# Layers two and three of a Fourier tower: where a pair's forward column transform stands among its products

## The reference, cut to what matters

```python
for i in range(nl):                                   # nl = 4
    h_ft = jnp.fft.rfft2(h)
    w_c = spec_wr[i] + 1j * spec_wi[i]
    out_modes = jnp.einsum('bixy,ioxy->boxy', h_ft[:, :, :mx, :my], w_c)   # 16 x 16 modes
    spec = jnp.fft.irfft2(out_modes, s=(H, W))
    conv = lax.conv_general_dilated(h, conv_w[i], (1, 1), 'SAME', dimension_numbers=dn)
    conv = conv + conv_b[i][None, :, None, None]
    h = leaky(spec + conv)
```

## Time and profile before

| | |
|---|---|
| median of 3 runs | 1116.0 us (1110.08, 1116.0, 1121.34) |
| the profiled execution's own time | 1121.72 us |
| span in its profile, first to last instruction | 1119.6 us |
| TensorE busy (matmul) | 1052.7 us, 94% |
| VectorE, ScalarE, GpSimd busy | 603.7, 466.2, 152.8 us |
| mean granted TensorE clock | 0.99 |

### The profile page before, as it was taken

The page is one execution under the profiler, slowest core; times in us unless marked ns, Lnnn a source line. Parts: engine busy times, 40 slices in busy tenths (PEclk is TensorE's granted clock), DMA queues, the critical chain, the costliest instruction groups (busy, mean ns, idle before and its releaser), DMA issues.

```text
span 1119.6 us, 48730 instructions
## 1 busy us (share of the span) xinstructions
PE 1052.7 (94%) x22512; PEld 553.4 (49%) x22512; DVE 603.7 (54%) x560; ACT 466.2 (42%) x895; POOL 152.8 (14%) x299
## 2 busy tenths in 40 slices
PE   5899999899999999899999998999999999899985
PEld 2555554555555554545544555434434344466743
DVE  5677788655556666555555665301233213387844
ACT  3355665223333333133333342223453534666524
POOL 2012221011111111011111110112102121200000
PEclk9999999999999999999999999999999999999998
DMA  9298889379888988588989887578757463000001
GB/s 321 62 206 209 211 189 256 106 213 272 252 254 257 267 212 241 150 243 222 269 251 261 241 236 191 135 171 193 179 143 167 102 142 83 7 4 1 1 1 19
DMA packets 66714, 194.27 MB, mean 174 GB/s; under 512 B 22256, under 2 KB 24816, under 8 KB 59248
## 3 DMA queue, kind: packets, MB, share of 16 engines
q1 hardware_dynamic: 54224, 138.19, 46.4%
q0 software_dynamic: 12288, 52.97, 17.3%
HBM read 138.13 MB, written 52.95 MB: 171 GB/s over the span
## 4 chain that ended last, share of the span: by engine, by line
PE 86%; DVE 6%; issue 4%; ACT 3%; DMA 0%; DVEq 0%; ACTq 0%
PE psum L662 16%; PE psum L648 15%; PE psum L694 12%; PE psum L676 7%; PE psum L633 5%; PE psum L620 5%; PE psum L566 4%; PE psum L553 4%; PE psum L712 3%; PE psum L605 2%; PE psum L908 2%; PE psum L720 1%; PE psum L760 1%; DVE xt L1288 1%; PE psum L926 1%
## 5 line engine op out<-in xcount | busy, mean ns | idle before, releaser
L1097 ACT ACTIVATE x_now<-psum,conv_bias 128x512 f32<-128x512 f32 x256 | 157.0, 691 | 340.3 <-PE psum L676 252.8
L1317 DVE STREAM_TRANSPOSE vt<-psum 128x1024 f32<-128x1024 f32 x64 | 126.2, 1972 | 195.1 <-PE psum L620 195.1
L1288 DVE STREAM_TRANSPOSE xt<-x_now 128x1024 f32<-128x1024 f32 x100 | 199.3, 2031 | 15.4 <-ACT x_now L1097 8.9
L1294 DVE STREAM_TRANSPOSE ft<-psum 128x1024 f32<-128x1024 f32 x50 | 100.8, 2016 | 194.0 <-PE psum L553 194.0
L662 PE MATMUL psum<-halo,conv 64*32 64x512 f32 x3072 | 188.3, 593 | 4.2 <-issue 4.2
L648 PE MATMUL psum<-halo,conv 128*128 128x512 f32 x384 | 179.7, 609 | 0.8 <-ACT x_now L1097 0.7
L497 POOL DMA_DIRECT2D activations<-x_now x192 | 94.3, 492 | 601.2 <-PE psum L662 411.6
L346 ACT ACTIVATE spec<-psum 32x128 f32<-32x128 f32 x372 | 143.7, 386 | 72.5 <-PE psum L566 68.7
L694 PEld LDWEIGHTS psum<-dft,vt 64*64 64x64 f32 x8192 | 130.3, 135 | 78.4 <-issue 77.1
L694 PE MATMUL psum<-dft,vt 64*64 64x64 f32 x8192 | 146.0, 221 | 4.4 <-issue 4.4
L648 PEld LDWEIGHTS psum<-halo,conv 128*128 128x128 f32 x384 | 69.0, 190 | 86.5 <-issue 78.1
(11 more groups left out here) (158 smaller groups left out, 793.7 us busy)
## 6 DMA issues: line engine op xcount, KB each, us to landing
halo<-activations SPq DMA_DIRECT2D x768, 132.0 KB, 3.5
activations<-x_now POOLq DMA_DIRECT2D x192, 264.0 KB, 4.1
wspec<-in_spec SPq DMA_DIRECT2D x64, 256.0 KB, 5.5
xcol<-in_xcol SPq DMA_DIRECT2D x16, 384.0 KB, 5.3
x_now<-in_ser SPq DMA_DIRECT2D x2, 1024.0 KB, 6.9
spec<-in_onehot SPq DMA_DIRECT2D x8, 256.0 KB, 5.7
wspec<-in_causal SPq DMA_DIRECT2D x8, 256.0 KB, 6.4
consts<-in_tail SPq DMA_DIRECT2D x6, 185.0 KB, 5.6
```

What stands on the lines that cost most here:

```text
L1097: copy(x_now[:, k, 16 * u:16 * u + 16, 0:G], acc[u].rearrange("p (i j) -> p i j", j=G), ACT.Prelu, bias=conv_bias[:, l:l + 1], alpha=SLOPE ...
L1288: vec.transpose(xt[:, 32 * m:32 * m + 32, :], src).then_inc(s_xt, 1)
L1317: vec.transpose(vt[:, k].rearrange("p h r o -> p (h r) o").rearrange("p y o -> p o y"), backed.rearrange("p a b -> p (a b)").rearrange("p ...
```

## The change

In `pair`, `columns_forward(T)` is issued after the second of the four centre products of pair `T` itself, from pair 2 on; the call at the end of the preceding pair is gone. At the boundaries into layers 2 and 3 it stands after the second centre product too, as it did at the boundary into layer 1. On ScalarE `spectrum` of a pair now stands ahead of the evictions of the pair in which its columns are computed, and no longer behind the evictions of the pair before; only the layer's last one keeps its old place. The number of instructions on each engine is unchanged, and no DMA, SyncE or GpSimd instruction is edited.

```diff
@@ -813,8 +813,10 @@
                     for part in range(4):
                         spectral(T, part)
                     return
-                for u in units(T):
+                for i, u in enumerate(units(T)):
                     convolve_centre(T, u)
+                    if p > 1 and i == 1:
+                        columns_forward(T)
                 for part in range(4):
                     spectral(T, part)
                 convolve_rows(T, 0)
@@ -824,7 +826,6 @@
                 convolve_columns(T, 1)
                 if p < LAST:
                     columns_back(T + 1)
-                columns_forward(T + 1)
 
             def last_pair(p):
 
@@ -858,7 +859,7 @@
                 T = l * PAIRS
                 for i, u in enumerate(units(T - 1)):
                     convolve_centre(T, u)
-                    if l == 1 and i == 1:
+                    if i == 1:
                         columns_forward(T)
                 rows_forward(T + 1)
                 convolve_rows(T, 0)
@@ -1176,7 +1177,7 @@
                         if u == 2:
                             fronts(p, 1)
                         head_activate(p - 1, u)
-                if l == 0 and p > 1:
+                if not last and p > 1:
                     spectrum(T - 2)
                 for u in units(T):
                     evict(T, u)
@@ -1187,7 +1188,7 @@
                     head_activate(p, 1)
                 if last:
                     fronts(p, 2)
-                if not last and (p > 0 if l > 0 else p == LAST):
+                if not last and p == LAST:
                     spectrum(T - 1)
                 if p == LAST and not last:
                     last_spectrum(T)
```

## The result

Over 20 runs of each kernel the changed one has a median of 1121.21 us (1117.76 to 1127.87) against 1116.99 us (1109.27 to 1123.04). The ratio is 1.0042 with a 95% interval of 1.0026 to 1.0058: 4.7 us more, between 2.9 and 6.5. The forecast was 6.5 us more, and 1122.5 us. The profiled execution took 1121.34 us, with a span of 1119.2.

The account below looks back on a forecast made before the run. TensorE, busy 94% and never waiting inside pairs, was taken as the bound. Splits (5.6 us) plus boundary waits (0.9) made +6.5 us on a median of 1116.0, so 1122.5 us, range 1115 to 1130.

Parts of the forecast that it names:

- TensorE waits for nothing in a pair, so there is no wait to win.: Pair ends of layers 1 and 2: ft is ready 0.34 us early, so 28 pair ends have no wait to remove.
- One more split costs 0.20 us.: Pairs 2 to 15 of two layers: a second run of whole-array products adds 0.20 us a pair, 5.6 us in all.
- The term L620 to L648: In a pair, columns_back before the first centre product: no change from 1.01 us, judged by L620 to L633 at 1.02.
- the second rival: Entering whole-array products from L620 costs another 0.20 us a pair: 12.1 us more, 1128 us, over 1% slower; chance 0.14.
- Evictions, `vt`, copies and `rows_forward` have time in hand in the pairs.: Inside pairs: no new waits, with at least 0.9 us in hand for evictions and 4 us for rows_forward.
- The boundaries make a wait of 0.44 us each.: Boundaries into layers 2 and 3: rows_forward waits for spec and starts 0.44 us later, 0.9 us for both.
- `convolve_columns` to the first centre product: Boundary into layer 2: 1.71 us plus 0.15 for the change of shape, placing the first centre product at 437.70.
- The sum, +6.5 us.: Whole kernel: 5.6 us from the pairs plus 0.9 from the boundaries, 0.6% up.
- Lateness of the pairs is untouched, since nothing that I could name moves it.: Layers 1 and 2: 17.2 us of unexplained lateness stays; the first rival (around 1117 us, chance 0.24) included losing a third.

Follow-up runs that it names:

- two_splits: Against the kernel before, forward columns cut in two halves, behind the second and third centre products, boundaries as before: ratio 1.0133, clean pair 14.26 us.
- extra: Kernel before plus one unused 64-column product behind the second centre product, pairs 2 to 15: same tile shape 1.0046, other shape (32 weight columns) 1.0094.
- no_split: Against the kernel before, forward columns put behind all four centre products of the pair's own list, boundaries as before: ratio 1.0240, clean pair 13.73 us.
- behind_spectral: Against the kernel before, forward columns put behind the four spectral parts, ahead of convolve_rows: ratio 1.0211, shortest clean pair 13.8 us.

## Why the prediction was right, point by point

- *TensorE waits for nothing in a pair, so there is no wait to win.* Held: the pair is 13.93 us, no shorter anywhere.
- *One more split costs 0.20 us.* Held to the hundredth in the changed kernel (13.93 us a pair), and `two_splits` scales it (0.53 for 0.58). That the 0.20 is the change of shape holds for the difference of the two `extra` runs; 0.12 us of another kind of break cost stands beside it, which the prediction didn't have. The term L620 to L648, which no row of before showed, was taken at 1.02 and measured 1.01; the second rival, which hung on it, falls.
- *Evictions, `vt`, copies and `rows_forward` have time in hand in the pairs.* Held; no such wait appears in pairs 2 to 15 of any kernel that changes layers 1 and 2.
- *The boundaries make a wait of 0.44 us each.* The mechanism was right, with `spec` ending 1.45 us of idle time, and the size was 0.53. The mis-sized term is `convolve_columns` to the first centre product: taken as 1.71 + 0.15, measured 1.94. Together 1.1 us, not 0.9.
- *The sum, +6.5 us.* From the measured terms it is 28 x 0.20 + 2 x 0.53 = 6.7; the runs say 4.7 (2.9 to 6.5), so the measured terms add up to a little more than the interval allows, and the forecast stands at its upper edge.
- *Lateness of the pairs is untouched, since nothing that I could name moves it.* This was the weak step, and it came out right by luck of the place. I had counted 17.2 us of it and treated it as noise that might shift. It isn't noise: some two thirds of it (10.0 of 14.6 us in 26 pairs) are instruction blocks that arrive late, and part of the 4.8 us between the layers is one pair of layer 2 with a pause of 2.24 us and the half clock behind it. Two other places for the same block raise the total by over 20 us (`no_split`, `behind_spectral`). In the changed kernel two long products stand on either side of the columns, so the short blocks are spread, and that keeps the lateness at the old size. Less of it would explain 4.7 in place of 6.7, but the windows (14.6 against 15.4) are one execution each and don't show as much.
- *ScalarE.* The edit there only follows the loop: before, the copies for pair `T + 1` stood behind the evictions of `T`, and now they stand ahead of the evictions of `T + 1`, which is the same place in its list.

## What to carry to other kernels

Where an engine is never idle, a block that is moved can only lose: count the runs of equal tile shape before and after, at 0.2 us for every one more, and read the price from starts of blocks and not from busy time or the modelled ends. Count also what lies next to what. Here TensorE's instructions came in blocks of 256 (127 matmuls with their weight loads), never less than 3.28 us apart; where short matmuls run through a block faster than that, it pauses at the border, so an order with equal or better pitch on paper can be 2% slower. Put long products between short ones. A pause that ends with `issue` is checked by its place in the list and by the packets of the instruction queue. And a wait that hangs on a third engine (columns, ScalarE's copies, `rows_forward`: 4.45 us) goes with the block to every new place; check it wherever the distance gets shorter.

## What the runs showed of the hardware that was not expected

- TensorE pauses for up to 2.3 us at the borders of its instruction blocks (256 instructions, one packet of 16,384 bytes): all 183 pauses over 0.2 us in 13 traces stand there and end 1.2 to 1.7 us after the packet. With no long products ahead they last 1.90 us in the mean of eight, with 1.06 us of them 0.61 us.
- Behind a pause of some 2 us the granted clock can fall to half; such a pair took 3.8 to 4.0 us more, about twice the pause (six pairs of layers 1 and 2, in three traces).
- A single short product (two records of 64 columns) of the same tile shape amid long ones costs 0.23 us, about twice its streaming time of 0.11 (estimated from 0.43 us for 512 columns); with 32 weight columns in place of 128 it costs 0.43.
- Three parts of spectral take 1.88 us when a part stands right behind the one whose end it waits for, and 1.58 with another part between: some 0.3 us. TensorE's matmuls show no idle time there; its weight loads do (0.23 us).
